# An attention layer unrolled over its tiles, with its start reordered

## The reference

```python
q, k, v = x @ Wq, x @ Wk, x @ Wv
q, k = rotate(silu(q)), rotate(silu(k))
# for each sequence, over its 4 chunks of 128 rows, carrying a state S (32 x 32 per head):
scores = (q_i @ k_i.T) * D
o = scores @ v_i + (q_i * decay_q) @ S
S = lam_C * S + (k_i * decay_k).T @ v_i
gate = x @ Wg1 @ Wg2
o = group_rmsnorm(o * sigmoid(gate)) * weight
out = o @ Wo
```

## Time and profile before

| | |
|---|---|
| median of 3 runs | 1410.6 us |
| profiled execution, its own time | 1410.67 us |
| its span (first to last instruction) | 1408.8 us |
| instructions | 18942 |
| mean granted TensorE clock | 0.99 |
| attention, first to last tile | about 0 to 345 us |

### The profile page before, as it was taken

How to read it: one execution, slowest core, us unless ns; L and a number is a source line. 1 busy time by engine, 2 the same in 40 slices (tenths; PEclk the granted TensorE clock), 3 DMA queues, 4 the chain that set the end, 5 groups by cost and what they waited for, 6 DMA issues and landing times.

```text
span 1408.8 us, 18942 instructions
## 1 busy us (share of the span) xinstructions
PE 1362.9 (97%) x7120; PEld 1127.5 (80%) x7120; DVE 1054.0 (75%) x1684; ACT 419.1 (30%) x669; POOL 248.1 (18%) x138
## 2 busy tenths in 40 slices
PE   5799999998899999999999999999999999999998
PEld 4678888886788888888888888888888888888886
DVE  7788878887776867777686868677776768686844
ACT  4334333332322222222222322222222222222221
POOL 3234434333110101011010101010101101011100
PEclk9899999999999999999999999999999999999999
DMA  9000000000010100010010101000000000000002
GB/s 314 23 1 16 2 16 0 15 1 1 1 42 19 30 16 30 16 30 30 15 30 15 30 16 43 15 30 15 30 15 30 30 15 30 15 30 16 1 30 90
DMA packets 21760, 40.20 MB, mean 29 GB/s; under 512 B 2644, under 2 KB 2900, under 8 KB 21588
## 3 DMA queue, kind: packets, MB, share of 16 engines
q1 hardware_dynamic: 20624, 39.08, 8.6%
q10 hardware_dynamic: 1092, 0.53, 0.2%
HBM read 35.40 MB, written 4.19 MB: 28 GB/s over the span
## 4 chain that ended last, share of the span: by engine, by line
PE 91%; DVE 5%; issue 1%; DMA 1%; ACT 1%; SPq 0%; DVEq 0%; ACTq 0%
PE bank L918 28%; PE bank L919 28%; PE bank L920 28%; PE bank L932 2%; PE bank L1001 1%; PE bank L1018 1%; PE bank L1107 1%; DMA w_in<-wk_dram 1%; PE bank L1008 1%; PE bank L1029 1%; DVE x1l L741 0%; DVE bst L505 0%; PE bank L968 0%; PE bank L967 0%; DVE nt_t L498 0%
## 5 line engine op out<-in xcount | busy, mean ns | idle before, releaser
L918 PE MATMUL bank<-x1h,wh 128*128 128x512 f32 x1024 | 398.7, 389 | 0.0
L920 PE MATMUL bank<-x1h,wl 128*128 128x512 f32 x1024 | 398.5, 389 | 0.0
L919 PE MATMUL bank<-x1l,wh 128*128 128x512 f32 x1024 | 398.5, 389 | 0.0
L851 POOL TENSOR_TENSOR wl<-wf,wh 128x1024 fp32r<-128x1024 f32 (+1 forms) x48 | 114.9, 2395 | 853.2 <-ACT wh L375 853.2
L918 PEld LDWEIGHTS bank<-x1h,wh 128*128 128x128 f32 x1024 | 192.4, 188 | 40.0
L920 PEld LDWEIGHTS bank<-x1h,wl 128*128 128x128 f32 x1024 | 192.2, 188 | 39.9
L919 PEld LDWEIGHTS bank<-x1l,wh 128*128 128x128 f32 x1024 | 192.2, 188 | 39.8
L778 DVE SCALAR_TENSOR_TENSOR hx<-hx,bank 128x512 f32<-128x512 f32 x128 | 88.0, 688 | 154.8 <-ACT hx L453 154.8
L918 PE MATMUL bank<-wh,hh 128*128 128x512 f32 x512 | 200.2, 391 | 3.2 <-DVE x1l L741 3.2
L919 PE MATMUL bank<-wl,hh 128*128 128x512 f32 x512 | 200.0, 391 | 0.0
L920 PE MATMUL bank<-wh,hl 128*128 128x512 f32 x512 | 199.9, 390 | 0.0
(11 more groups left out here) (108 smaller groups left out, 1490.5 us busy)
## 6 DMA issues: line engine op xcount, KB each, us to landing
pk<-packed_dram SPq DMA_DIRECT2D x48, 256.0 KB
sc<-scales_dram SPq DMA_DIRECT2D x48, 256.0 KB
out_dram<-acc SPq DMA_DIRECT2D x16, 256.0 KB, 2.2
acc<-x_dram SPq DMA_DIRECT2D x3, 1024.0 KB, 14.1
w_in<-wq_dram SPq DMA_DIRECT2D x2, 512.0 KB, 4.6
w_in<-wk_dram SPq DMA_DIRECT2D x2, 512.0 KB, 10.0
w_in<-wv_dram SPq DMA_DIRECT2D x2, 512.0 KB, 14.6
maskT<-mask_dram SPq DMA_DIRECT2D x1, 1024.0 KB, 11.7
```

The costliest lines, as they stand in the source:

```text
L851: nc.gpsimd.tensor_tensor(wl[par][:, bass.ds(u, 1), :].rearrange("p a w -> p (a w)"), wf[:].rearrange("p a w -> p (a w)"), wh[par][:, bass ...
L918: pe.matmul(dst, w_h, x_h, start=start, stop=False)
L919: pe.matmul(dst, w_h, x_l, start=False, stop=False)
L920: return pe.matmul(dst, w_l, x_h, start=False, stop=stop)
```

## The change

- `batches` has no loop: tiles 0 to 15 are all written out.
- SyncE loads input tiles 0 and 1 first (one DMA each), then Wq, the first gate weight, Wk, Wv, the second gate weight, the rotation table, tiles 2 and 3, sequence 1, the norm weight, Wo and then the tables. ScalarE issues the identity only.
- Statistics: tiles 0 and 1 first; 2 to 7 in one job after xt_lo(1); 8 to 15 in twos, at two places each of tiles 1 and 2; their `stats_r` in tile 3.
- The v weight's low part goes from GpSimd to VectorE. The second gate weight's split goes behind it.
- Tile 1's x is transposed into bank BO, ahead of tile 0's v products (it was BV, behind them).
- `wo_hi`, `norm1(2)`, tanh/silu and gate low part of tile 1 go ahead of tile 0's q and k copies; `wo_lo` goes ahead of tile 0's gating.
- Units: bits at tiles 4, 6, 8; scale at 5, 7, 9; high and low parts at 6, 8, 10.
- TensorE multiplies cleared data (`st`, float32, 128x512) four times at its start and twice after the first transposes. The results are overwritten.

```diff
 def batches(eng, body, last_tile):
-            for c in range(CHUNKS):
-                body(0, c)
-            with eng.Fori(1, BATCH - 1) as b:
-                for c in range(CHUNKS):
+            for b in range(BATCH):
+                for c in range(CHUNKS - (b == BATCH - 1)):
                     body(b, c)
-            for c in range(CHUNKS - 1):
-                body(BATCH - 1, c)
             last_tile()
...
+            for t in range(2):
+                sp.dma_start(acc[:, t, :], xv[:, t, :]).then_inc(s_xt0, 16)
             load_w(0, 0)
+            sp.dma_start(g1_in, wg1...).then_inc(s_small, 16)
             load_w(1, 1)
             load_w(2, 2)
+            sp.dma_start(g2_in, wg2...).then_inc(s_small, 16)
+            sp.dma_start(rotT[:], rot).then_inc(s_rot, 16)
+            sp.dma_start(acc[:, 2:CHUNKS, :], xv[:, 2:CHUNKS, :]).then_inc(s_x[0], 16)
+            load_x(1)
+            sp.dma_start(nw[:], norm_w).then_inc(s_nw, 16)
+            sp.wait_ge(s_whi, 2)
+            sp.wait_ge(s_wlo, 2)
+            load_w(3, 0)
             (tables dqT, dkT, lamT, maskT; then load_x(2), load_x(3))
...
+            norm1(1, 1)                  # ScalarE prologue, after Wk's high parts
             g1s copy; weight_hi(2, 2, 0); weight_hi(2, 2, 1)
+            g2s copy                     # was before weight_hi(2)
             tanh_qk(0); gate_low(0); v_copy(0, 0); xt_hi_(1); tanh_gate(0)
+            wo_hi()
+            norm1(2, 3)
+            tanh_qk(1)
+            gate_low(1)
...
-            dve.wait_ge(s_xt0, 16)
-            stats(0, 1)
-            stats_r(0, 1, 0)
+            dve.wait_ge(s_xt0, 32)
+            stats(0, 2)
+            stats_r(0, 2, 0)
...
+            weight_lo(2, 2, 0)
+            weight_lo(2, 2, 1)
...
             xt_lo_(1)
+            dve.wait_ge(s_x[0], 16)
             dve.wait_ge(s_x[1], 16)
-            stats(CHUNKS, 2 * CHUNKS)
-            stats_r(CHUNKS, 2 * CHUNKS, 2)
+            stats(2, 2 * CHUNKS)
+            stats_r(2, 2 * CHUNKS, 1)
+            silu_qk(1)
+            gate_low(1)
...
+                if t in (1, 2):          # VectorE, after decayed_q(t)
+                    dve.wait_ge(s_x[t + 1], 16)
+                    stats(4 * t + 4, 4 * t + 6)
+                if t in (1, 2):          # after add_x1(t - 1)
+                    stats(4 * t + 6, 4 * t + 8)
+                if t == 3:
+                    stats_r(2 * CHUNKS, TILES, 2)
...
+            pe.wait_ge(s_st0, 1)
+            for n in range(4):
+                pe.matmul(BO[:], st[:, 0, :], st[:].rearrange("p k t -> p (k t)"), start=True, stop=True)
             pe.wait_ge(s_id, 16)
             x_transpose(0)
+            for n in range(2):
+                pe.matmul(BO[:], ...)    # the same product
             pe.wait_ge(s_wlo, 1)
             q_ready(0)
...
             k_project(0)
+            pe.wait_ge(s_glo, 1)
+            gate1(0)
+            x_transpose(1)
+            v_project(0)
             pe.wait_ge(s_glo, 2)
-            gate1(0)
-            v_project(0)
-            x_transpose(1)
             gate2(0)
```

More of the change, by code:

```diff
@@ L330, in xt_hi_ @@
                 act.wait_ge(v_ps, t)
-                A(xth[:], BV[:].rearrange("p (k t) -> p k t", k=KT), ACT.Copy).then_inc(xt_hi, 1)
+                src = BO if isinstance(t, int) and t == 1 else BV
+                A(xth[:], src[:].rearrange("p (k t) -> p k t", k=KT), ACT.Copy).then_inc(xt_hi, 1)
             def gate_low(t):
@@ L405, in tile @@
                 if not near_end(b, c, 1):
-                    tanh_qk(t + 1)
-                    gate_low(t + 1)
+                    if not at_start(b, c):
+                        tanh_qk(t + 1)
+                        gate_low(t + 1)
                     v_copy(t + 1, (c + 1) % 2)
@@ L413, in tile @@
                 if not near_end(b, c, 3):
[L414 to L417, removed]
+                    norm1(t + 3, 3 if t + 3 < 2 * CHUNKS else 5)
                 ot_copy(t)
                 square(t)
-                if c == 0 and not (isinstance(b, int) and b == 0):
-                    unit_hi(b - 1, b - 1, 0)
+                if t in UNIT_PARTS:
+                    unit_hi(UNIT_PARTS.index(t), UNIT_PARTS.index(t), 0)
             def x1t_hi_(t):
@@ L538, in xt_lo_ @@
                 dve.wait_ge(xt_hi, t + 1)
-                V.tensor_tensor(xtl[:], BV[:].rearrange("p (k t) -> p k t", k=KT),
+                src = BO if isinstance(t, int) and t == 1 else BV
+                V.tensor_tensor(xtl[:], src[:].rearrange("p (k t) -> p k t", k=KT),
                                 xth[:].bitcast(F32), ALU.subtract).then_inc(xt_lo, 1)
@@ L633, in stats2 @@
                 dve.wait_ge(ln2_done, last)
-                newton(s_ntl, ln2[:, rows, 1], last - first, r2[:, rows], NT * (4 + n), 1.0,
+                newton(s_ntl, ln2[:, rows, 1], last - first, r2[:, rows], NT * (3 + n), 1.0,
                        LN_EPS)
@@ L694, in tile @@
                 decayed_q(t)
-                if c == 2 and not near_end(b, c, 4):
-                    unit_bits_a(b, b, [32] * UNITS)
+                if t in (1, 2):
+                    dve.wait_ge(s_x[t + 1], 16)
+                    stats(4 * t + 4, 4 * t + 6)
+                if t in UNIT_BITS:
+                    unit_bits_a(UNIT_BITS.index(t), UNIT_BITS.index(t), [32] * UNITS)
                 if not near_end(b, c, 1):
-                    silu_qk(t + 1)
-                    gate_low(t + 1)
+                    if not at_start(b, c):
+                        silu_qk(t + 1)
+                        gate_low(t + 1)
                     rope_of(b, c, t + 1, (c + 1) % CHUNKS)
@@ L707, in tile @@
                     add_x1(t - 1)
[L708 to L711, removed]
+                if at_start(b, c):
+                    wo_lo()
+                if t in (1, 2):
+                    stats(4 * t + 6, 4 * t + 8)
+                if t == 3:
+                    stats_r(2 * CHUNKS, TILES, 2)
+                if t in UNIT_BITS:
+                    unit_bits_b(UNIT_BITS.index(t), UNIT_BITS.index(t))
+                if t in UNIT_SCALE:
+                    unit_scale(UNIT_SCALE.index(t), UNIT_SCALE.index(t))
                 gated(t)
@@ L884, in tile @@
                     decay_k_(b, c + 1, t + 1)
-                if c == 0 and not (isinstance(b, int) and b == 0):
-                    unit_lo(b - 1, b - 1, 0)
+                if t in UNIT_PARTS:
+                    unit_lo(UNIT_PARTS.index(t), UNIT_PARTS.index(t), 0)
             def norm2(t):
@@ L936, in x_transpose @@
                 pe.wait_ge(xn_done, t + 1)
+                if isinstance(t, int) and t == 1:
+                    transposes(BO, xn).then_inc(xt_ps, 1)
+                    return
                 pe.wait_ge(v_sb, t)
@@ L973, in v_project @@
                 first = isinstance(t, int) and t == 0
-                project(BV, 2, (s_vlo, 1) if first else None).then_inc(v_ps, 1)
+                project(BV, 2, (s_wlo, 5) if first else None).then_inc(v_ps, 1)
             def gate2(t):
@@ L1037, in x1_transpose @@
                 transposes(BX[t], wf[:, t % 2, :]).then_inc(x1t_ps, 1)
+            pe.wait_ge(s_st0, 1)
+            for n in range(4):
+                pe.matmul(BO[:], st[:, 0, :], st[:].rearrange("p k t -> p (k t)"), start=True,
+                          stop=True)
             pe.wait_ge(s_id, 16)
             x_transpose(0)
+            for n in range(2):
+                pe.matmul(BO[:], st[:, 0, :], st[:].rearrange("p k t -> p (k t)"), start=True,
+                          stop=True)
             pe.wait_ge(s_wlo, 1)
```

42 lines of the change are left out of this document (8 added, 34 removed).

## The result

Four runs gave 1396.35 to 1397.18 us, median 1396.72, against 1410.57 before: ratio of the times after and before 0.9903 (95% interval 0.9885 to 0.992). That is 13.9 us less, where 16.5 were forecast. The profiled execution has a span of 1395.1, that is 13.7 less.

The account below looks back on a forecast made before the run. TensorE, busy 97% of the span, was taken as the bound, with idle or slow time to win only ahead of 101.2 us. 8.2 + 8.8 - 0.5 = 16.5 off 1410.6 gave 1394.1 us, range 1390 to 1398.

Parts of the forecast that it names:

- The load order: Prologue: Wk's second half lands at 13.6 us (bounds 12 and 15), Wv at 16.2 (bounds 15 and 19.2).
- Wv's low part: from its landing to the low part of tile 1's x at 23.5: Prologue, VectorE: chain from Wv's landing at 16.2 ends at 23.5 instead of 30.18, 6.7 us earlier.
- Scores(0) 8.2 us earlier: Prologue: tile 0's scores start at 35.2 instead of 43.37, behind VectorE's root at 30.8; bounds 5 and 10.5.
- a rival for the first products: Prologue, part of the 0.15 rival: zeros don't raise the clock, first products run slow, silu(0) 3.8 us later.
- From scores to tile 1's transposes as before, 11.3: Tile 0: the old chain keeps its 11.3 us, so tile 1's transposes start at 46.5 instead of 54.71.
- Tiles 1 to 3, 8.8: Attention tiles 1 to 3: 56.4 us instead of 65.2 with bn_stats spread in twos; 8.8 gained, bounds 6 and 9.3.
- The units, -0.5: Tiles 4 to 11: bits and scale cost nothing, moved unit_lo loses 0.5 us; bounds -1 and +4.
- the cleared products, 0: Kernel start: zeros may raise the clock early, but later waits remain; 0 us, bounds -1 and +4.
- A: Rival, chance 0.15: prologue gains little, as Wv lands late or zeros don't raise the clock; 1399 us.
- B: Rival, chance 0.08: VectorE becomes the bound in tiles 1, 2 or 7 to 9; 1398 us.
- D: Rival, chance 0.05: no gain, scores(0) no earlier than 43, tiles' excess has another cause; 1410 us.
- E: Rival, chance 0.05: written-out tiles cost instruction fetches, some 9 more at 3 us, 28 us lost; 1422 us.

Follow-up runs that it names:

- the run with the split semaphore: Changed kernel with a semaphore of its own for the second gate weight, so ScalarE's first gate-weight copy no longer waits for that load: 1394.39 us, ratio 0.9878.
- fills: Kernel with the second gate weight's own semaphore, plus TensorE idle stretches filled with fp32r products whose results are overwritten: 1391.42 us, ratio 0.9871 against the kernel before.

## Why the prediction was right, and where it was off

The direction, the place (all ahead of tile 4) and the range held. The forecast of 1394.1 was 2.6 us low. The mechanism was right for tiles 1 to 3 and wrong in the prologue: the prediction names scores(0) behind 40 as a sign that it is wrong, and they are at 40.25. That the sum still came near is partly luck, as the stretch behind the scores gave back 2.1 us that it did not hold. By its steps:

- *The load order.* Mis-sized the other way. Wv was taken to land at 16.2; it was there by 13.5 to 14.5 (its high parts run back to back from 13.54 in the run with the split semaphore), and Wk's high parts started at 11.1, not 13.6. The ninth load's issue did not stall. (Counted in the trace, it was the tenth load that had stood 4.22 us before, not the ninth.)
- *Wv's low part: from its landing to the low part of tile 1's x at 23.5.* This step failed. It ended at 26.98. What stands in its place is a wait that the code before had too and that was free there: ScalarE's wait for both gate weights. I followed VectorE's queue past the moved load, and not ScalarE's, and gave the second gate weight no landing time at all. With that wait taken away, the chain comes out at 24.0, by two errors that cancel: Wv's low parts end 1.4 us before the 18.5 of the sum, and then everything waits for the second gate weight, until 17.87.
- *Scores(0) 8.2 us earlier.* It was 3.1, in the run without the wait 7.3. I had VectorE's root as the last thing ahead of tanh of tile 1. It was ready at 33.5; TensorE's k products ended later, at 35.8, because the 14 products from 27.16 ran at the lower clock and took 2.8 us more. TensorE needed 13.1 us from the q products to the scores, where the sum had 10.3 with every product at 0.235. The rows before already showed the q products of tile 1 start slowly behind a wait (0.77 at 30.37). The clock was in my sum only as a rival for the first products. So the 5.1 us that scores(0) are later than forecast are 3.7 for the later q products and 2.8 for the clock, less the 1.4 by which TensorE's sum had stood below VectorE's.
- *From scores to tile 1's transposes as before, 11.3.* It was 9.2. The rotation now runs ahead of the first scores (masks start 1.2 us behind them, not 2.0), and the products behind the masks kept the upper clock (1.08 and 1.16 us instead of 1.93 and 1.66). That gave back 2.1, which I did not foresee.
- *Tiles 1 to 3, 8.8.* 7.9. The cause as given is shown for 5.3 of it. Another 1.4 are Wo's low parts, costed at nothing, and 0.6 probably the unit bits that left tile 2. Tile 1 stayed 0.9 long. The lower bound of the prediction names its pairs of bn_stats as a reason for that; the record points at Wo's low parts as well. They took 3.52 us, not 2.7, and the gating behind them began at 47.88, some 1.3 us after TensorE's transposes back had ended.
- *The units, -0.5.* The sign was wrong: a gain of 1.1 by the run that puts them back. Between the two kernels it is -0.2 in tiles 4 to 12 and +0.4 in tile 13, which no unit_lo precedes any more. The 2.27 us Newton instruction stands at the start of tile 7, as foretold:

```profile
162.08 2.27 DVE L491 TENSOR_SCALAR nt_v<-ms 128x16 f32<-128x16 f32 x1
```

- *The loop, 0; the cleared products, 0.* Both shown by a run of their own.

Of the rivals, A (the prologue gains little) is what happened in part, by a mechanism that it did not name. B was seen only in tile 1 (0.9 of its 2.5 us). D and E fell, as did B for tiles 7 to 9: no tile of 4 to 12 grew by over 0.5 us.

Left open: why a wait of 2.5 us costs more clock in one execution than in the next, and what 0.6 us of the gain in tiles 1 and 2 were. Also not separated is the gain of 5.3 us ahead of tile 1: no run puts back the load order, the one job of statistics for tiles 2 to 7, or the order of tanh and norm on ScalarE. The single edits that were put back there (Wv's low part, tile 1's transposes, cleared products) carry 0.5 us, an unknown part and nothing.

## What to carry to other kernels

When a load is moved back, look for every wait that counts it, also those that share its semaphore, and then at what is queued behind the waiting instruction: here one copy of a small weight held a large one for 4 us. Small jobs of an engine that is 80 to 90% busy belong one at a time, into waits that its own trace shows; a block of 4.8 us of bn_stats cost 3.9 us of one tile, even though the engine is idle for part of every tile. Where TensorE must wait two to four microseconds, products whose results nobody reads can pay, as they keep its clock for what comes next; at the very start, with a later wait for Wv's low part to hide it, they paid nothing.

## What the runs showed of the hardware

- TensorE's waits differ in what they cost of its granted clock. Behind the 3.5 us in the last tile the products were slow in all eleven profiles without fills (the scores took 2.09 us in the changed kernel, 1.17 with fills). Behind the 2.5 us ahead of q of tile 1, 8 to 14 products were slow in six profiles of seven. Behind the 1.6 us in tile 14 the clock fell in four profiles of the thirteen; the tile then took 19.1 to 19.3 us instead of 17.7.
- The clock column can show 1.00 where products run at the lower level. It does so from 10.57 to 16.6 us of the kernel before, though the products there start 0.43 us apart. There the level is read from that spacing.
- Float32 products of zeros raised the clock too: with them the q products are at the upper level from 13.5, without them from 15.9.
- A float32 product of 512 columns took about 1.7 us at the lower clock (four in 6.74 us, in the run with the split semaphore) and 0.94 at the upper (a pair in 1.88).
- The unrolled loop of some 300 TensorE instructions a tile cost and gained nothing (ratio 1.0003, 0.9993 to 1.0013).
